# Pass 0 of a graph network kernel: 74 of its 104 edge groups gathered, two runs of destinations summed from count blocks instead

## The reference, cut to what matters

```python
# pass 0, then a two-layer MLP with batch norm
h = segment_sum(x[src], dst) + x
h1 = relu(batch_norm(h @ W1 + b1))             # W1: 256 x 1024
x1 = layernorm(x + relu(h1 @ W2 + b2))         # W2: 1024 x 256
# passes 1 to 3: graph layers, norm = dinv[src] * dinv[dst], deg counts the edges of a node
h = relu(segment_sum((h @ W.T)[src] * norm, dst) + b)
out = layernorm(x1 + h)
```

## Time and profile before

| | us |
|---|---|
| median of 3 runs | 3627.93 (3625.74 to 3635.08) |
| profiled execution, span from first to last instruction | 2930.2 |
| median less span | 697.7 |
| pass 0, to the first MLP matmul | 1119.5 |

### The profile page before, as it was taken

The page is one execution under the profiler, slowest core; times in us unless marked ns, Lnnn a source line. Parts: engine busy times, 40 slices in busy tenths (PEclk is TensorE's granted clock), DMA queues, the critical chain, the costliest instruction groups (busy, mean ns, idle before and its releaser), DMA issues.

```text
span 2930.2 us, 44233 instructions
## 1 busy us (share of the span) xinstructions
PE 2390.3 (82%) x15784; PEld 1770.1 (60%) x15784; DVE 1427.8 (49%) x3556; ACT 956.0 (33%) x1512; POOL 2020.2 (69%) x2141
## 2 busy tenths in 40 slices
PE   3676666766666678999999987899998889999986
PEld 2444444444444447776777765677776667777754
DVE  7787777678677775760223233122222321424234
ACT  0111111111111115554444433444444334344431
POOL 6777777777777760017777777677777757777774
PEclk9988878888878888999999999999999999999998
DMA  4444554555454446987889898779898977888894
GB/s 136 141 159 143 162 161 141 161 160 161 143 160 159 144 148 219 344 305 251 296 297 308 285 330 297 242 255 307 298 311 297 312 235 245 298 275 285 272 315 127
DMA packets 360951, 680.17 MB, mean 232 GB/s; under 512 B 44051, under 2 KB 190441, under 8 KB 354827
## 3 DMA queue, kind: packets, MB, share of 16 engines
q0 software_dynamic: 102576, 295.31, 32.3%
q10 hardware_dynamic: 154688, 222.02, 22.6%
q1 hardware_dynamic: 103451, 159.81, 15.4%
HBM read 559.42 MB, written 117.51 MB: 231 GB/s over the span
## 4 chain that ended last, share of the span: by engine, by line
PE 60%; DVE 17%; DMA 9%; issue 7%; DVEq 2%; ACT 2%; POOL 0%; SPq 0%; ACTq 0%; POOLq 0%
PE ps L1074 30%; PE ps L938 8%; PE ps L976 6%; PE ps L920 6%; DVE vreg L1263 5%; PE ps L986 4%; DMA hbuf<-parts_d 4%; DMA xs<-in_x_dram 3%; PE ps L950 2%; DVEq L1220 2%; DVE vreg L1250 1%; DVE vreg L1244 1%; PE ps L963 1%; DMA xs<-x_d 1%; ACT strips L679 1%
## 5 line engine op out<-in xcount | busy, mean ns | idle before, releaser
L632 POOL DMA_INDIRECT ring<-table_d,idx x1236 | 1183.6, 958 | 437.7 <-issue 375.4
L1074 PE MATMUL ps<-wide,hbuf 128*128 128x512 f32 x4116 | 1039.7, 404 | 38.0 <-DMA hbuf<-parts_d 32.1
L632 POOL DMA_INDIRECT ring<-in_x_dram,idx x832 | 821.0, 987 | 264.0 <-issue 251.6
L1074 PEld LDWEIGHTS ps<-wide,hbuf 128*128 128x128 f32 x4116 | 760.4, 191 | 262.5 <-issue 60.7
L792 ACT CAST wide<-abuf 128x1024 fp32r<-128x1024 uint8 (+1 forms) x588 | 552.5, 940 | 633.3 <-PE ps L1074 632.6
L1216 DVE TENSOR_TENSOR acc<-acc,ps 128x256 f32 x260 | 107.5, 413 | 663.8 <-PE ps L938 662.5
L920 PE MATMUL ps<-ring,hot 128*32 128x256 f32 x4136 | 317.4, 429 | 101.1 <-issue 82.7
L950 PE MATMUL ps<-vreg 128*128 128x300 bf16 x840 | 197.3, 345 | 231.0 <-DVE vreg L1263 212.2
L938 PE MATMUL ps<-place,strips 128*128 128x128 f32 x2068 | 317.9, 303 | 64.7 <-ACT strips L679 34.6
L938 PEld LDWEIGHTS ps<-place,strips 128*128 128x128 f32 x2068 | 295.1, 214 | 105.9 <-ACT strips L679 55.8
L1263 DVE TENSOR_TENSOR vreg<-vreg,ps 128x600 f32 x420 | 329.4, 784 | 54.4 <-DVE vreg L1263 23.6
(11 more groups left out here) (131 smaller groups left out, 1541.2 us busy)
## 6 DMA issues: line engine op xcount, KB each, us to landing
hbuf<-parts_d ACTq DMA_DIRECT2D x84, 1024.0 KB
hbuf<-parts_d ACTq DMA_DIRECT2D x84, 768.0 KB
abuf<-ad_d ACTq DMA_DIRECT2D x63, 896.0 KB
parts_d<-vreg SPq DMA_DIRECT2D x72, 512.0 KB, 7.2
h_d<-ureg SPq DMA_DIRECT2D x23, 1024.0 KB, 7.3
ureg<-h_d POOLq DMA_DIRECT2D x23, 1024.0 KB, 8.2
ad_d<-vreg SPq DMA_DIRECT2D x28, 784.0 KB, 4.2
ring<-table_d,idx POOLq DMA_INDIRECT x1236, 4.9
```

The costliest lines, as they stand in the source:

```text
L632: pool.indirect_dma_start(out=ring[:, i % SLOTS, j, :], out_offset=None, in_=table[0:N, :], in_offset=at).then_inc(g["rows"][i % SLOTS], 16)
L1074: ins = pe.matmul(ps[:, 2 + 4 * q + h, 0:(n1 - 4 * q) * P].rearrange("p (s n) -> p s n", n=P), hbuf[:, bl, e * D + h * P:e * D + (h + 1) * P],
```

## The change

Pass 0 gathers only the 74 groups that are not in the first two dense runs (`SPARSE0`). These two runs, of eight windows each, are cut into four "quads" of four windows. Their blocks are built first (240 tiles at the positions 2 to 36 of 74), read back from `ad_d`, and multiplied in `dense_step0` with rows of x that were split into `parts[1]` earlier in the pass: 4 x 49 dense steps of four matmuls, in positions 12 to 64. The other 180 tiles follow at the positions 37 to 73. The 30 groups that are not gathered still count their edges ("light" groups: `light_strips`, `light_sums`, `keep_counts`, `add_counts`).

Blocks are built for pairs of source blocks: a uint16 column holds the count for the one block in its low byte and for the other in its high byte, so the second one-hot is multiplied by 1 or 256 (`weight`), the product has 300 columns in one matmul, and the add covers 300 elements instead of 600. `lohot` is made for two tiles in one instruction. Two blocks (`aclear`) take turns, and ScalarE clears them. The ring has three slots in pass 0 (SLOTS0; the fourth holds `split0`), `hs` is used by one half but for one chunk, chunks retire in another order (ORDER0 = 4, 5, 11, 0, 12, ...), and one list PLAN sets the order of all five engines.

```diff
+        work = [("strips", s, 0)] + [("own", TURN0[c], 0) for c in AT0[s][:1]] + one_step() + [("sums", s, 0)]
+        work += [("lstrips", s, 0)] * len(LIGHT_AT[s]) + one_step() + [("lsums", s, 0)] * len(LIGHT_AT[s])
+        for c in AT0[s]:
+            if c != AT0[s][0]:
+                work.append(("own", TURN0[c], 0))
+            for pr in range(HP):
+                work += [("hidden", TURN0[c], pr)] + one_step()
+        work += [("dense", k, 0) for k in steps]
+        more = [("part", c, 0) for c in PARTS_AT[s]] + [("tile", t, 0) for t in TILES_AT[s]]
+        behind = [[] for _ in work]
+        for n, m in enumerate(more):
+            behind[(2 * n + 1) * len(work) // (2 * len(more))].append(m)
+        PLAN.append([x for w, ms in zip(work, behind) for x in (w, *ms)])
...
+            def load_part(c):
+                u = c % 2
+                wait(sp, s_part, 2 * (c - 1))
+                sp.dma_start(tile_of(xparts, u, c), rows_of(x, c)).then_inc(s_partl[u], 16)
+
+            def store_part(c):
+                u = c % 2
+                sp.wait_ge(s_part, 2 * (c + 1))
+                halved = split0[:, u, :, :, :].rearrange("p b e d -> p b (e d)")
+                sp.dma_start(rows_of(parts[1], c), halved if c < NCH else halved[0:REM, 0, :]).then_inc(s_partst[u], 16)
+
+            def load_quad(m):
+                j, c = m // DLOADS, m % DLOADS
+                d, q = RUNS0[j]
+                blocks_stored(sp, FIRST0[j] + QUAD)
+                wait(sp, s_wide0, (m - 1) * BLOCKS)
+                sp.dma_start(quads[:, m % 2, :, :], ad_d[d, :, QUAD * q:QUAD * (q + 1), pairs(c)]).then_inc(s_quad[m % 2], 16)
+
+            def load_row(k):
+                b = k % NB
+                wait(sp, s_step0, k - QUAD + 1)
+                sp.dma_start(hbuf0[:, k % QUAD, :].bitcast(F32), parts[1][b * P:(b + 1) * P, :]).then_inc(s_row[k % QUAD], 16)
...
+                if pr == 0 and v == 0:
+                    wait(act, s["hst"], 16 * min(r, NCH - 1))
...
+            def widen0(k):
+                m, bl = k // BLOCKS, k % BLOCKS
+                if bl == 0:
+                    act.wait_ge(s_quad[m % 2], (m // 2 + 1) * 16)
+                wait(act, s_step0, k - 1)
+                act.copy(wide0[:, k % 2, :, :], one_block(quads[:, m % 2, :, :], m % DLOADS, bl)).then_inc(s_wide0, 1)
...
             def build(t):
                 pe.wait_ge(s_oh, t + 1)
                 wait(pe, s_ba, t - 1)
-                for e in range(2):
-                    ins = pe.matmul(ps[:, BUILDBANK[t % 2] + e, 0:JW // 2], lohot[:, t % TB, :], jhot[:, t % TB, e * JW // 2:(e + 1) * JW // 2],
-                                    start=True, stop=True)
-                ins.then_inc(s_bm, 1)
+                pe.matmul(ps[:, BUILDBANK + t % 2, 0:JW], lohot[:, t % TB, :], jhot[:, t % TB, :],
+                          start=True, stop=True).then_inc(s_bm, 1)
+
+            def dense_step0(k):
+                j, b = k // NB, k % NB
+                pe.wait_ge(s_row[k % QUAD], (k // QUAD + 1) * 16)
+                pe.wait_ge(s_wide0, k + 1)
+                if b == 0:
+                    wait(pe, s_dacc0, QUAD * j)
+                for e in range(HALVED):
+                    for h in range(DH):
+                        ins = pe.matmul(ps[:, 6 + h, :].rearrange("p (s n) -> p s n", n=P),
+                                        hbuf0[:, k % QUAD, e * D + h * P:e * D + (h + 1) * P], wide0[:, k % 2, :, :],
+                                        start=(b == 0 and e == 0), stop=(b == NB - 1 and e == HALVED - 1))
+                ins.then_inc(s_step0, 1)
...
             def tile_hot(t):
                 at, j = t // TILES, t % TILES
-                wait(dve, s_bm, t - TB + 1)
-                dve.tensor_scalar(lohot[:, t % TB, :], iotal, lot[:, at, j:j + 1], None, ALU.is_equal)
-                dve.tensor_scalar(jhot[:, t % TB, :], iotaj, keyt[:, at, j:j + 1], None, ALU.is_equal).then_inc(s_oh, 1)
...
+                wait(dve, s_bm, t - TB + 2 - t % 2)
+                if t % 2 == 0:
+                    dve.tensor_tensor(lohot[:, t % TB:t % TB + 2, :], lot[:, at, j:j + 2].unsqueeze(2).to_broadcast([P, 2, P]),
+                                      iotal.unsqueeze(1).to_broadcast([P, 2, P]), ALU.is_equal)
+                dve.tensor_scalar(jhot[:, t % TB, :], iotaj, keyt[:, at, j:j + 1], weight[:, at, j:j + 1],
+                                  ALU.is_equal, ALU.mult).then_inc(s_oh, 1)
...
+                wait(dve, s_partst[u], 16 * (c // 2))
+                t, upper, rest = xparts[q, u, 0:nb, :], split0[q, u, 0:nb, 0, :], split0[q, u, 0:nb, 1, :]
+                step(dve.tensor_scalar(upper.bitcast(I32), t.bitcast(I32), UPPER, None, ALU.bitwise_and))
+                dve.tensor_tensor(rest, t, upper, ALU.subtract).then_inc(s_part, 1)
```

More of the change, by code:

```diff
@@ new lines, in gnn_kernel, with one_step @@
+    assert not HALFRUNS or (sum(PARTS_AT, []) == list(range(NCH + 1)) and not any(PARTS_AT[READY0 - 1:]))
+    PLAN = []
+    for s in range(NS0):
+        steps = iter(STEPS0[s])
+        def one_step():
+            return [("dense", k, 0) for k in itertools.islice(steps, 1)]
+        work = [("strips", s, 0)] + [("own", TURN0[c], 0) for c in AT0[s][:1]] + one_step() + [("sums", s, 0)]
[11 more added lines that the diff above has]
+        PLAN.append([x for w, ms in zip(work, behind) for x in (w, *ms)])
@@ L377, in gnn_kernel @@
         NCH1 = NCH + 1
[L380 to L381 removed]
+        STATS_AT = list(range(NS0 - 2 - HT, NS0 - 2))
+        WELL = len(sum(AT0[:STATS_AT[0]], []))
         EVEN, ODD = NCH // 2 + 1, NCH // 2
@@ new lines, in add_quad @@
+            def add_quad(j, n):
+                starts = columns(bases, FIRST0[j], QUAD, N - 1)
+                dve.wait_ge(aggs[0]["acc"], n)
+                dve.wait_ge(s_step0, (j + 1) * NB)
+                for m, g in enumerate([*range(0, QUAD, 2), *range(1, QUAD, 2)]):
+                    if g == 1:
+                        dve.wait_ge(s_dacc0, QUAD * j + m)
+                    to = acc[:, :, bass.ds(starts[g], P)]
+                    dve.tensor_tensor(to, to, ps[:, 6:8, g * P:(g + 1) * P], ALU.add).then_inc(s_dacc0, 1)
+                dve.wait_ge(s_dacc0, QUAD * (j + 1))
@@ L1409, in _ @@
             dve.drain()
-            for k in EVERY:
-                if k + 1 < NG:
-                    make_hot(0, k + 1, k + 1)
-                for t in EARLY_AT[k]:
-                    add_tile(t)
-                add_group(0, k, k)
-                if k == 0:
+            starts, done = [], 0
+            for i, work in enumerate(PLAN):
+                light = LIGHT_AT[i]
+                if i == BEGIN:
+                    flag = regular(dve)
+                    tile_hot(0)
+                    tile_hot(1)
+                for what, n, pr in work:
+                    if what == "strips":
+                        if light:
+                            make_hot(0, LITEM[i], light[0], True)
+                        elif i + 1 < NS0:
+                            make_hot(0, ITEM[i + 1], SPARSE0[i + 1])
+                    if what == "sums":
+                        add_group(0, i, SPARSE0[i])
+                        done = ITEM[i] + 1
+                        if light:
+                            make_hot(0, ITEM[i + 1], SPARSE0[i + 1])
+                    if what == "lsums":
+                        add_counts(i, light[0])
+                        done = LITEM[i] + 1
+                    if what == "part":
+                        make_part(n)
+                    if what == "tile":
+                        if n + 2 < NT:
+                            tile_hot(n + 2)
+                        add_tile(n, starts)
+                    if what == "dense" and n % NB == NB - 1:
+                        add_quad(n // NB, done)
+                    if what == "hidden":
+                        if pr == 0:
+                            hidden_in(fast[0], n, (aggs[0]["acc"], ITEM[i] + 1))
+                        hidden_out(fast[0], n, pr)
+                if i == 0:
                     step = order(dve, s_key)
```

525 lines of the change are left out of this document (326 added, 199 removed).

## The result

| | before | after | ratio |
|---|---|---|---|
| median us of 4 runs each | 3630.55 (3625.74 to 3635.08) | 3422.91 (3410.37 to 3430.77) | 0.943 (0.9397 to 0.9464) |
| the same two kernels on another chip, 7 and 4 runs | 2933.25 (2929.02 to 2938.43) | 2814.55 (2809.63 to 2826.8) | 0.9588 (0.9568 to 0.9608) |

The account below looks back on a forecast made before the run. Gathers bound pass 0 before, TensorE mostly afterwards: 214 + 682 + 22 + 20 + 9.6 = 948 us against 1119.5. With 8 us added behind it, 3627.9 - 163.5 = 3464 us, range 3325 to 3590.

Parts of the forecast that it names:

- The gathers set the pace before, and TensorE's list after: Pass 0: 832 gathers at 1.295 us bound it before; afterwards TensorE needs 10.6 to 11.4 us a position, over 10.36.
- TensorE's busy time: Pass 0, TensorE: terms sum to 743 to 788 us, times an overlap factor of 0.915 gives 680 to 721.
- TensorE busy for 0.924 of the positions 12 to 73: Pass 0 after the front: 610 to 651 us of TensorE work at this share takes 660 to 705 us.
- The front, position 12 at 214 us: Start of pass 0: position 2 at 78 us, eight VectorE-bound positions of 14.7 us, then 18 us for positions 10 and 11.
- One half of `hs`, 22 us: Eleven chunks in pass 0 wait for the previous chunk's store, 0 to 4 us each, 2 taken.
- Rows late, 20 us: Pass 0 dense steps: rows of x, loaded three steps ahead in SP's queue, land late; 0 to 160 us, 20 taken.
- Later passes +8 us: Behind pass 0: block loads read eight blocks instead of seven, 9.6 MB more; 0 us hidden, 29 not, 8 charged.
- The 697.7 us, left as they are: Whole run: the timed median lies 697.7 us above the profiled span, unexplained, and was kept unchanged in the forecast.
- That they shrink in proportion: Rival, whole run: the 697.7 us shrink too, so 202 us of gain instead of 163.5, 3425 us; chance 0.08.
- The gathers as the bound: Rival, pass 0: TensorE packs better than 0.924, gathers stay the bound, 300 us less, 3335 us; chance 0.12.
- The 27 us from calmer gathers: Side of the gathers' rival, pass 0: less VectorE interference saves at most 45 ns a gather over 592 gathers.
- The lists hold each other up: Rival, positions 12 to 73: TensorE and VectorE wait for each other, 1.5 us more a position, 3557 us; chance 0.17.

Follow-up runs that it names:

- spread_both: Changed kernel with parts spread among tiles, rows loaded from ScalarE's queue four steps ahead, dense steps in TensorE's waits: ratio 0.94 on a slow chip, 0.9323 on a quick one.
- after_ref: The changed kernel again, unchanged, timed and profiled on a quick chip: ratio 0.9588 to the kernel before.
- no_dense0: Changed kernel with HALFRUNS = 0, so pass 0 gathers all 104 groups and has no dense steps: 3587.63 us against 3593.97 before, ratio 0.9971, slow chip.
- wide_counts: Changed kernel with the degree counts of four strips in one matmul of 128 weight columns instead of four of 32: 2831.53 us, ratio 0.9661, quick chip.

## Why the prediction was right, and where it was off

Forecast 3464 us in a range of 3325 to 3590; measured 3422.91. The side and the range held. But 163.5 us of gain were made out of a quick chip's trace and set against a slow chip's median, and neither chip gave that: 118.7 on the quick, 207.6 on the slow one. That 3464 came within 41 us is in part luck: on the kind of chip whose trace was used the gain was over-estimated by 45 us, and what the slow chip gave beyond it was no term of the sum. The steps are judged on the quick chip, whose trace they used.

- **The gathers set the pace before, and TensorE's list after.** Held: 190.7 us of POOL's waits for TensorE.
- **TensorE's busy time.** Strips (93.0 us) and sums (93.6) lay within their bounds. Dense steps took 242.3 us for 198.6, builds 134.1 for 98.7, hidden columns 206.7 for 188.9: all the terms together 855 us for 743 to 788, too low. The union was 730.2 us from 28 us on, for 680 to 721, since records overlapped more: a factor 0.854 and not 0.915. That the positions 12 to 73 came out at 630.93 us, within the 610 to 651, is two errors that offset each other. Ahead of them, from 28 to 241.5 us, TensorE was busy 97.6 us where the prediction had about 70.
- **TensorE busy for 0.924 of the positions 12 to 73**, taken from the later passes: it was 630.93 / 741.5 = 0.851, and 0.92 in clock, not 0.97. With the 22 and 20 us for two waits the forecast had 724 us; it was 741.5, 17.5 more. Of the waits that make it the largest was not named at all, 38.8 us for VectorE's sum of own rows, and the 23.4 us ahead of the light counts the prediction had only as a rival.
- **The front, position 12 at 214 us**: the step that failed most. It began at 241.5 us, 27.5 later. Position 2 began 6.5 us earlier than forecast and took as much longer and more, so position 3 was close (92.7 forecast, 95.4 measured); the seven with stalls took 118.1 us for 102.9, of which some 8 are the chunk at position 7; the two behind took 28.1 for 18, the chunk at 11. The sum charged chunks to TensorE's busy time and nothing to the front, though TensorE is at its lower clock there (3.78 us for the first eight hidden matmuls at position 7, 1.89 for eight at its end). The chunks make some 19 of the 27.5 us, and the positions 3 to 6, at 17.0 us for 14.7, another 9; what made those longer is open. The stalls of the parts were 2.0 to 4.9 us a position, 32.3 in all (3.7 and 29.6 forecast), their mechanism right to the line, and with the parts spread 4.5 us were left.
- **Sizes on VectorE**: add of 300 columns 468 ns (451), wide one-hot 355 (323), pair 413 (402), in the slow chip's trace. Near enough.
- **One half of `hs`, 22 us**: too high. TensorE waited 2.5 us for it on the quick chip, 9.4 on the slow one.
- **Rows late, 20 us**: 28.4, of which 9.0 at the very first step, whose loads are issued only in position 12 (from 244.3 us). With them on another queue, one step further ahead, 8.8. The DMA share from 78 us to the end of the pass was 0.70 for a forecast 0.76, so the engines were shared without being full. By the Trainium skill ("DMA: Bandwidth & Descriptors", "Issuing engines are not separate DMA queues"), transfers run on the same 16 engines whichever engine issued them, so another queue alone buys little; the run changed the queue and the distance together, and doesn't separate them.
- **Later passes +8 us**: +21.7 on the quick chip, inside the bounds of 0 and 29.
- **The 697.7 us, left as they are**: wrong in kind. They lie inside the span of a slow chip, most of them as waits. That they shrink in proportion was a rival with 3425 us, near the measured figure by luck: it would give one ratio on both kinds of chip, and they gave 0.943 and 0.9588. In pass 0 the slow chip's surplus went from 281.6 us (1401.1 - 1119.5) to 219.5 (1212.1 - 992.6), 2.7 and 3.0 us a position, as if fewer positions met fewer late signals. But with spread_both it is 1223.8 - 907.0 = 316.8, 4.3 a position, so it is no fixed price. Between the two kinds I can say where the difference lies, not its law.
- **The other rivals.** The gathers as the bound fell (190.7 us of waits for TensorE). The 27 us from calmer gathers too: they took 987 ns in the mean before and 987 in `after_ref`, so less work on VectorE gave nothing back. The Trainium skill ("SBUF — State Buffer", "SBUF: two separate sides") has VectorE's two-port forms lock GpSimd out; no effect of that on the gathers shows in this trace. "The lists hold each other up" was true in part: 17.5 us over the forecast instead of 93.

So on the quick chip the prediction for the span was 2767 us and 2824.9 was measured: 27.5 for the front, 17.5 for the positions behind, 13.7 for the later passes, less 0.8 of rounding.

## What to carry to other kernels

Work that is put into an engine's idle time in a line of waits is not free because the engine is a third idle: here each dense step, with all that came with it, cost three quarters of what its matmuls last. Where it stands in the list may matter as much as how long it is: with steps put where TensorE waited for VectorE, rows asked for earlier and the parts spread, the cost fell to two fifths on a quick chip, though which of these gave how much behind the front was not run apart, and on a slow chip the first two gave nothing. When several loads with two buffers feed work on an in-order list, put other work between them: the third in a row stops everything behind it, and spreading them took 27.8 of 32.3 us of stalls away and made the front 31.5 us shorter. And compare the profiled execution's own time with the timed runs before subtracting anything: a trace from one chip and a median from another are two baselines.

## What the runs showed of the hardware that was not expected

Two kinds of chip, 22 to 24% apart on one program (2930 and 2933 us; 3594, 3627 and 3631), with the same duration of single instructions (gathers 946 and 947 ns in the median, strip copies 585 and 586) and different waits: on the slow kind the readers of TensorE's signals start together some 5 us late in many positions, with no releaser in the trace; ScalarE's strip copies wait 808.2 us in 121 such cases over the kernel before, and in none on the quick kind. Such waits occur with and without the dense steps (658.8 us up to 1200 us in `no_dense0`). The cause is open; no run changed the number of signals or the traffic alone, and each kind was told by its times and waits, not by anything known of the chips. A change is worth different amounts on the two kinds, 0.9588 and 0.943, and an edit can be worth nothing on one and 2 to 3% on the other.

Also: a record of a one-column fp32 matmul with 128 weight columns was busy for 164 ns (`wide_counts`), while four records of narrow ones side by side together take 77 ns (`after_ref`).
